# One program for layer 0's feed-forward stage and layer 1's attention

## What is computed

```python
x = layernorm(x + L0_attn(x))     # causal softmax attention
x = layernorm(x + L0_ffn(x))      # ternary weights, silu(x Wu^T) * (x Wg^T), then Wd
x = layernorm(x + L1_attn(x))     # see below
x = layernorm(x + L1_ffn(x))      # silu gate, float32 weights

def L1_attn(x):                   # 16 query heads, 4 key/value heads
    cw = sigmoid(sum(abs(x), axis=-1))
    q = (x * cw) @ Wq
    k, v = split(x @ Wkv)         # keys and values repeated 4 times
    s = q k^T / 4 + alibi(head, -|i-j|)
    s = where(allowed, -1e9, s)   # allowed: |i-j| <= 32, or i < 64, or j < 64
    return softmax(s) v @ Wo + bo
```

## Time and profile before

| | us |
|---|---|
| median of 3 runs (1118.72 to 1123.28) | 1122.21 |
| time of the profiled execution | 1118.5 |
| its span | 1116.8 |
| PE busy in it | 996.9 (89%) |
| DVE busy | 704.0 (63%) |
| ACT busy | 600.9 (54%) |
| POOL busy | 341.0 (31%) |
| mean granted clock of PE | 0.969 |

### The profile page before, as it was taken

How to read it: one execution, slowest core, us unless ns; L and a number is a source line. 1 busy time by engine, 2 the same in 40 slices (tenths; PEclk the granted TensorE clock), 3 DMA queues, 4 the chain that set the end, 5 groups by cost and what they waited for, 6 DMA issues and landing times. The chain is left out here.

```text
span 1116.8 us, 17952 instructions
## 1 busy us (share of the span) xinstructions
PE 996.9 (89%) x6546; PEld 519.4 (47%) x6546; DVE 704.0 (63%) x1549; ACT 600.9 (54%) x1184; POOL 341.0 (31%) x405
## 2 busy tenths in 40 slices
PE   7678999999988999665799999999999999899995
PEld 4332333333334888542233343433333344698885
DVE  2877777778725565466878787777777734225322
ACT  4335666676665334241357777777777676423320
POOL 3031322221211444400252543525234251324331
PEclk9898999999999999977889999999999999999998
DMA  7552120111000000042451331303021000000001
GB/s 248 165 170 68 58 58 16 44 58 58 2 2 1 1 1 1 1 164 66 138 171 41 119 121 40 122 1 122 22 101 36 1 1 1 1 1 20 19 1 38
DMA packets 32979, 64.19 MB, mean 57 GB/s; under 512 B 6079, under 2 KB 22351, under 8 KB 30516
## 3 DMA queue, kind: packets, MB, share of 16 engines
q1 hardware_dynamic: 31004, 58.07, 16.7%
q0 software_dynamic: 1072, 3.80, 1.0%
q10 hardware_dynamic: 816, 1.18, 0.3%
HBM read 50.45 MB, written 12.32 MB: 56 GB/s over the span
## 5 line engine op out<-in xcount | busy, mean ns | idle before, releaser
L932 ACT ACTIVATE prob<-ps 128x512 f32<-128x512 f32 (+6 forms) x896 | 442.8, 537 | 214.8 <-PE ps L978 207.1
L978 PE MATMUL ps<-qop,kop 98*128 98x512 bf16 (+15 forms) x1376 | 302.5, 291 | 21.1 <-ACT prob L932 7.6
L964 PE MATMUL ps<-kop,qop 96*128 96x512 bf16 (+3 forms) x896 | 255.5, 358 | 40.7 <-DVE maxes L871 21.1
L978 PEld LDWEIGHTS ps<-qop,kop 107*128 107x128 bf16 (+2 forms) x1376 | 114.4, 98 | 278.1 <-ACT prob L932 200.9
L1005 PE MATMUL ps<-prob,vst 128*32 128x512 f32 (+4 forms) x1792 | 211.2, 543 | 3.9 <-POOL prob L810 2.6
L871 DVE CUSTOM_DVE_ANT_0 sums<-ps,tri 128x128 bf16<-128x128 f32 (+7 forms) x256 | 183.7, 754 | 43.8 <-PE ps L964 42.5
L871 DVE CUSTOM_DVE_ANT_0 sums<-ps,alibi_table 128x960 bf16<-128x960 f32 x128 | 148.0, 1156 | 77.8 <-PE ps L964 63.4
L810 POOL TENSOR_TENSOR prob<-prob,keep 128x384 int32<-128x384 int32 (+2 forms) x144 | 122.8, 854 | 224.7 <-ACT prob L932 222.2
L1364 PE MATMUL ps<-xs,ffn_parts 128*128 128x512 f32 x640 | 150.4, 392 | 4.5 <-DVE hf L1338 2.3
L871 DVE CUSTOM_DVE_ANT_0 tri<-ps,alibi_table 128x960 bf16<-128x960 f32 x128 | 147.5, 1153 | 3.6 <-PE ps L964 3.6
L1364 PEld LDWEIGHTS ps<-xs,ffn_parts 128*128 128x128 f32 x640 | 119.0, 188 | 29.7 <-DVE hf L1338 3.1
(11 more groups left out here) (99 smaller groups left out, 682.6 us busy)
## 6 DMA issues: line engine op xcount, KB each, us to landing
alibi_table<-in_table SPq DMA_DIRECT2D x32, 464.0 KB, 5.0
qop<-q_parts SPq DMA_DIRECT2D x96, 128.0 KB, 2.7
kop<-k_parts SPq DMA_DIRECT2D x48, 128.0 KB, 2.6
kop<-k_parts SPq DMA_DIRECT2D x48, 96.0 KB
q_parts<-qop SPq DMA_DIRECT2D x8, 384.0 KB, 2.9
q_parts<-kop SPq DMA_DIRECT2D x8, 384.0 KB, 3.5
x<-in_x SPq DMA_DIRECT2D x4, 512.0 KB, 6.0
out<-x SPq DMA_DIRECT2D x4, 512.0 KB, 3.0
```

Of the source, the lines that this page charges most:

```text
L932: nc.scalar.activation(prob[0:rows, q % 2, k % HG, lo % CH:lo % CH + hi - lo], ps[0:rows, t_bank(n, k), lo % CH:lo % CH + hi - lo], ACT.Ex ...
L964: last = nc.tensor.matmul(ps[:, S_BANK + 2 * (k % S_SLOTS) + a // CH, a % CH:a % CH + b - a], qop[0:RD, par, h, i0:i0 + P], kop[0:RD, par, ...
L978: return nc.tensor.matmul(ps[0:rows, bank, a % CH:a % CH + b - a], lhs, rhs, start=start, stop=True, skip_group_check=True)
```

## The change

Layer 0's feed-forward stage and layer 1's attention become one block. `feed_forward` becomes a class `FeedForward` whose engine programs are called at the head of layer 1's attention block; its last down projection, the adding, the last inverse ("root") and the last normalisation ("normal") are steps of layer 1's opening, among the first six maxima. Batch 0 of layer 1's projection is spread behind units 14 to 30 by the dictionary `BRIDGE`, on banks 6 and 7; batch 1 has banks 4, 5 and 6. The order of the units changes too: keys and first query block of a chunk side by side.

The exp on ACT becomes a pow with base 1/e on POOL ("decay", with the 1 added there). For batch 1, "weigh" and "scale" are on ACT (activations Abs with an accumulator, and Copy with a scale). The memory plan is written out by hand (`memory`), so that both stages' buffers fit beside one another: the hidden buffer is four pieces, and xt, xct and vt are one for each batch. Layer 1's projection weights are loaded by SP instead of ACT, at the head of the block. SP's queue is now: weights, constants of buffer 0, (wait for the last gather of attention outputs) four tables, sends 0 to 3, load of group 0, sends 4 and 5, (last hidden tile) constants of buffer 1, (last subtraction) two tables, (last down projection) load of group 1, sends 6 to 11, and on as before. The third part of unit 5 is made at unit 6's step, as before.

```diff
@@ opening_of
+    else:
+        tail = [("down", 0), 0, 1, ("second", 0), ("down", 1), 2, 3, ("second", 1), ("root", 0), 4, 5, ("normal", 0)]
+        out = [maxima[step] if isinstance(step, int) else (*step, 0) for step in tail]
+        maxima = maxima[6:]
     for n, unit in enumerate(maxima):
         out.append(unit)
         upto = [-(-len(behind) * m // (len(maxima) - 2)) for m in (n, n + 1)]
...
+BRIDGE = {14: [("weigh", 0), ("decay", 0)],
+          16: [("divide", 0), ("scale", 0)],
+          20: [("turn", 0), ("turn", 1)],
+          21: [("turn", 2), ("turn", 3)],
+          22: [("weigh", 1), ("decay", 1), ("unit", 0)],
+          23: [("turn", 4), ("turn", 5), ("divide", 1), ("scale", 1)],
+          24: [("turn", 6), ("turn", 7)],
+          25: [("unit", 1)],
+          26: [("unit", 2)],
+          27: [("unit", 3)],
+          28: [("unit", 4)],
+          29: [("unit", 5)],
+          30: [("v", 0)]}
@@ Projection
+            orders = (((KD, 0), (0, 0), (KD, 1), (0, 1), (1, 0), (1, 1)), ((KD, 0), (0, 0), (1, 0), (KD, 1), (0, 1), (1, 1)))
+            self.units = [(b, m, c) for b in range(B) for m, c in orders[b]]
...
+        banks = ((4, 5, 6), (4, 5, 6)) if i == 0 else ((6, 7), (4, 5, 6))
...
+        u, t = units, turns
+        return [("weigh", 2), ("decay", 2), *t[:2], ("divide", 2), ("scale", 2), u[0], *t[2:4], u[1], ("weigh", 3), ("decay", 3),
+                *t[4:6], ("divide", 3), ("scale", 3), u[2], *t[6:], *u[3:], ("v", 1)]
...
+        if self.tenant[step] is not None:
+            self.wait_read(pe, *self.tenant[step])
+        elif self.before is not None and self.bank_of[step] < 6:
+            pe.wait_ge(self.before.prep.added[1], 2 * NC)
+        elif self.before is not None:
+            pe.wait_ge(self.before.prep.n_lo, KD * NC)
...
+        elif what == "decay":
+            tiles = slice(CT * k, CT * k + CT)
+            pool.wait_ge(self.weighed[k // 2], (CT * (k - 1)) if k >= 2 else k + 1)
+            nc.gpsimd.tensor_tensor(self.cw[:, 1, tiles], self.K.inverse_e[:], self.cw[:, 0, tiles], ALU.pow
+                                    ).then_inc(self.cw_exp, 1)
+            pool.wait_ge(self.cw_exp, 2 * k + 1)
+            nc.gpsimd.tensor_scalar(self.cw[:, 2, tiles], self.cw[:, 1, tiles], 1.0, 0.0, ALU.add, ALU.add
+                                    ).then_inc(self.cw_exp, 1)
@@ attend, SP
+                sp.wait_ge(before.prep.gathered, NC)
+                for g in range(HG):
                     load_table(g)
...
-            later = len(proj.units) // 2 + 2 + 2 * (1 - i)
+            later = len(proj.units) // 2 + 2 * (1 - i)
             for u in range(4, later):
                 proj.send(sp, u)
+            if i == 1:
+                sp.wait_ge(before.hid, NC * KE)
+                operands.constants(sp, 1)
+                sp.wait_ge(before.h_lo, NC * KE)
+                for g in range(HG, TABLES):
+                    load_table(g)
+                sp.wait_ge(before.down_full, 2 * NC)
             operands.load(sp, 1)
@@ attend, PE (the same call stands at the head of DVE's, ACT's and POOL's program)
+            if before is not None:
+                before.pe(pe)
             step(-1, opening)
             all_groups(step)
@@ FeedForward
+    def pe(self, pe):
+        self.unit(pe, 0)
+        self.unit(pe, 1)
+        for c in range(NC):
+            for u in range(c * KE + 2, min((c + 1) * KE + 2, NC * KE)):
+                self.unit(pe, u)
+            if c < NC - 1 or self.i == 1:
+                for half in range(2):
+                    self.down(pe, c, half)
...
+        for what, k in self.between(u):
+            self.prep.act(act, what, k)
+        for what, k in self.bridge(u):
+            self.proj.act(act, what, k)
```

More of the change, by code:

```diff
@@ L175, in opening_of @@
 def opening_of(layer, proj):
-    first = proj.steps(0)
+    maxima = [("max", u, 1) for u in range(len(units_of(layer)))]
     behind = proj.steps(1) + [("flush", 0)]
-    maxima = [("max", u, 1) for u in range(len(units_of(layer)))]
     if layer.index == 0:
+        first = proj.steps(0)
         for j, step in enumerate((("unit", 2), ("unit", 4), ("v", 2))):
@@ new lines, in dve_tail, with unit @@
+    def dve_tail(self, dve, what, k):
+        if what == "second":
+            self.add_second(dve, NC - 1, k)
+        elif what == "normal":
+            self.prep.normalise(dve, NC - 1, 1)
+    def unit(self, pe, u):
+        nc, ps, prep, pairs = self.nc, self.K.ps, self.prep, self.pairs
+        c, e = u // KE, u % KE
+        if e == 0 and c >= 2:
+            pe.wait_ge(prep.n_lo, KD * (c + 1))
+        for which, weights, full in ((0, self.wup, self.up_full), (1, self.wgate, prep.gate_full)):
+            if u >= 2:
+                pe.wait_ge(self.silu_done if which == 0 else self.hid, u - 1)
+            n = 0
+            for k in range(KD):
+                for a, b in pairs:
+                    last = nc.tensor.matmul(ps[:, 2 * (u % 2) + which, :],
+                                            weights[a][:, k, e * P:(e + 1) * P],
+                                            prep.xs[:, c % 2, b, k, :],
+                                            start=(n == 0), stop=(n == KD * len(pairs) - 1))
+                    n += 1
+            last.then_inc(full, 1)
+        for what, k in self.between(u):
+            prep.pe(pe, what, k)
+        for what, k in self.bridge(u):
+            self.proj.pe(pe, what, k)
@@ new lines, in down @@
+    def down(self, pe, c, half):
+        nc, pairs = self.nc, self.pairs
+        pe.wait_ge(self.h_lo, KE * (c + 1))
+        if c >= 1:
+            pe.wait_ge(self.prep.added[1], 2 * (c - 1) + half + 1)
+        for j in range(2 * half, 2 * half + 2):
+            n = 0
+            for e in range(KE):
+                for a, b in pairs:
+                    last = nc.tensor.matmul(self.K.ps[:, 4 + half, (j % 2) * D:(j % 2 + 1) * D],
+                                            self.hidden(e, b)[:, j * P:(j + 1) * P], self.wdown[a][:, e, :],
+                                            start=(n == 0), stop=(n == KE * len(pairs) - 1))
+                    n += 1
+        last.then_inc(self.down_full, 1)
@@ new lines, in pe, with pe_tail, alone, _ @@
+    def pe(self, pe):
+        self.unit(pe, 0)
+        self.unit(pe, 1)
+        for c in range(NC):
+            for u in range(c * KE + 2, min((c + 1) * KE + 2, NC * KE)):
+                self.unit(pe, u)
+            if c < NC - 1 or self.i == 1:
+                for half in range(2):
+                    self.down(pe, c, half)
+    def pe_tail(self, pe, what, k):
+        if what == "down":
+            self.down(pe, NC - 1, k)
+def alone(nc, ffn):
+    with ExitStack() as st:
+        block = st.enter_context(nc.Block())
+        @block.sync
+        def _(sp):
+            ffn.sync(sp)
@@ L1391, in _ @@
-            unit(0)
-            unit(1)
-            for c in range(NC):
-                for u in range(c * KE + 2, min((c + 1) * KE + 2, NC * KE)):
-                    unit(u)
-                down(c)
+            ffn.pe(pe)
 def one(n):
```

507 lines of the change are left out of this document (273 added, 234 removed).

## The result

| | kernel before | kernel after |
|---|---|---|
| median, first measurement (5 runs each) | 1121.93 us | 1106.43 us (1099.92 to 1107.78) |
| median, second measurement (9 and 5 runs) | 1122.16 us | 1102.68 us (1100.16 to 1103.88) |
| ratio to before, first | | 0.9853 [0.9832, 0.9875] |
| ratio to before, second | | 0.9825 [0.9805, 0.9845] |
| profiled execution | 1118.5 | 1099.92, span 1098.2, clock 0.973 |

The change makes the kernel faster, by 15.5 us in the first measurement and 19.5 in the second. A median of 1099 us with a range of 1089 to 1112 was predicted: sign and range hold, and the saving is 3.5 to 7.5 us smaller than the 23 forecast.

The account below looks back on a forecast made before the run. TensorE was taken as busy nearly everywhere but for one hole between feed-forward and maxima, the maxima as VectorE's. 29.7 us less up to the first maximum and 6.7 more in the maxima phase gave -23.0, a median near 1099 us, range 1089 to 1112.

Parts of the forecast that it names:

- Up to the first maximum: From unit 31's last matmul to the first maximum: 27.3 us in place of 57.0, so 29.7 us less.
- The stall before turn 6: Units 20 to 24: PE waits for the scaled tokens, 5.8 us of which 4.0 are covered, a stall of 1.8.
- the stall at turn 5: Units 20 to 24: turn 5 needs the bank of unit 0's projection, costing 0.8 us.
- the wait for the last hidden tile: Behind the last unit's matmul: hidden tile, rounding, subtraction and hand-offs hold PE up for 3.0 us.
- the down half: Half of the last down projection ahead of the first maximum: 4.0 us, with +4.0 as bound for half clock.
- The maxima phase: Group 0's maxima on DVE: 43.4 us of work and 6.7 of waits, 50.1 us, so 6.7 us more.
- About 0.35 at each of six units: Maxima phase: DVE waits about 0.35 us at each of six projection units, within the 6.7 us of waits.
- Operands late: Rival: third parts, scaling or sends held up, first maximum waits for "kop<-k_parts"; 15 us saved, 1107; chance 0.15.
- Chains exposed: Rival: each projection unit adds its whole chain to PE, each turn 0.7; 2 us saved, 1120; chance 0.03.
- slower, by the clock: Rival: stalls strewn over units 20 to 31 hold PE at 1.2 GHz; 32 us lost, 1154; chance 0.03.
- Table loads: Rival: ACT's Copy inside the Silu loop brings two loads of 1.28 at six units; 1111 us; chance 0.02.
- The prediction's 5.2 us: Bound on the operands' chain: four third parts could each wait out a POOL subtraction of 1.29; taken as 0.

Follow-up runs that it names:

- experiment 4: e3_flush_early: kernel after with unit 5's second and third part made ahead of the last down projection instead of at unit 6's step; 1102.2 us, 0.9833 to the kernel before.
- Experiments 2 and 3: e2_bridge_last, and that kernel with the whole last down projection, adding and normalisation also ahead of the maxima: 1108.54 us, 0.9894 to the kernel before.
- e1_tail_first: Kernel after with the last down projection, its adding, root and normalisation ahead of all maxima, bridge kept; 1108.11 us, 0.9884 to the kernel before.
- e7_three: Kernel after with unit 5's third part early, turns 6 and 7 one unit later, and chunk 2's normalisation behind the last hidden tile; 1096.2 us, 0.9773.
- e8_keep_busy: Kernel after with 38 idle transposes (20, 12 and 6) in waits of TensorE around the last down projection; 1101.93 us, 0.9829 to the kernel before.
- e2_bridge_last: Kernel after with batch 0's turns, projection units and value turn all behind unit 31, down projection still among the maxima; 1113.8 us, 0.9929 to the kernel before.
- e6_normal_late: Kernel after with chunk 2's normalisation moved from feed-forward unit 29 to the head of the opening; 1103.0 us, 0.9832 to the kernel before.

## Why the prediction was right, and where it was off

**Up to the first maximum: right.** 29.7 us were predicted. The two profiles of before with the slow start have 155.60 and 155.73 from the feed-forward's start to the first maximum, those of after 125.37 and 125.33: 30.3 less (28.4 less than the first profile of before, 153.76). Within it the terms moved both ways. The stall before turn 6 was 2.98 instead of 1.8, since the scaling took 1.92 us beside POOL, inside the bounds of 1.14 to 3.3; the stall at turn 5 (0.8) was absent; the wait for the last hidden tile was 3.64 instead of 3.0; the down half took 5.42 up to the first maximum instead of 4.0, on the way to the 8.0 of its bound for half clock. Against that the turns were cheaper: two in a row occupy PE for 0.79 (438.04 to 438.83), where I took 1.20 from the row's length, so 1.6 less over four pairs. A row's length overstates: the next row starts before it ends. Units 26 to 29 took 3.57 each against 3.7. The 0.9 us that are left of the balance are about the two waits of PE, 0.75 and 0.26 us, that the kernel before has inside unit 24 (at 433.24) and ahead of the down projection of chunk 2. In the kernel after they are gone, and the prediction had not counted them. Some 3.2 us were so put too low and some 4 us too high: that this part came out within 0.6 us is in part luck.

**The maxima phase: this is the step that failed.** "Together 6.7, so 50.1 us" was 54.5 (54.51 and 54.49 in the two profiles of after, against 43.46). DVE's waits in it are 10.15 instead of 6.7, and its work about 1 us more than 43.4. By its terms: the start 0.73 (0.6), the second down half 1.62 (2.2), three units in a row 1.60 (1.8) were right. "About 0.35 at each of six units" was not: the three units that stand apart cost 0.79, 2.56 and 0.80, 4.15 in place of 2.1. Three waits (0.39, 0.49, 0.49) for a maximum's product that stands behind four transposes at the lower clock were not in the sum. Nor was unit 5's third part, 0.68 waited and 0.69 of work, though the change's description says that it is made at unit 6's step; experiment 4 takes it out of the phase. Most of this was to be seen in the phase before: the lines above have waits of 0.38 and 0.49 and the third part there, and DVE waited 0.86 for the cast of the first unit. The prediction wrote that phase as maxima, remainders and "the rest waits", and then put new waits in the place of the rest instead of reading it.

Of the 4.4 us some 3 are rows at the lower clock (1.37 behind the transposes, some 1.8 of the 2.56), in a phase for which the prediction's own showed 0.89, while the sum took PE's durations at full clock. The 1.8 is no fixed price: of the eleven profiles of one-block kernels three (e1_tail_first, e7_three, e8_keep_busy) have no projection unit at the lower clock in this phase and eight have one or two, of 3.05 to 3.55 us, not always the same unit; the three of the kernel before have none.

**The rivals.** *Operands late* did not happen, though the first measurement's 1106.43 lies at its price (1107) and just outside the forecast's own range of 1094 to 1106: there is no wait for "kop<-k_parts". Unit 3's third part was done at 468.79, 12.8 us behind the end of chunk 2's down projection (13.3 predicted). Experiments 2 and 3 show that the mechanism is real when the bridge is later (5.24 and 1.76). *Chains exposed* and *slower, by the clock* were wrong as well: PE runs 447.9 to 474.9 without a gap at clock 1.00. *Table loads* in the silu loop there are none, and the one that moved is hidden, as the timeline of ACT in the kernel after shows:

```profile
534.99 1.28 ACT L1005 ACT_TABLE_LOAD   x1
```

It runs 6 us before the first exp's matmul at 542.31.

**The Trainium skill** ("SBUF — State Buffer", section "Who interferes with whom") says that a VectorE instruction with two SBUF inputs contends with a GpSimd instruction that reads SBUF, and that the order of issue decides which of the two is held up. The prediction's 5.2 us took only the case in which VectorE is. Two third parts met a subtraction of POOL, by the timeline of DVE in the kernel after,

```profile
457.98 0.78 DVE L485 TENSOR_TENSOR qop<-staging,qop 64x512 bf16<-64x512 f32 x1
...
462.83 0.67 DVE L485 TENSOR_TENSOR qop<-staging,qop 128x512 bf16<-128x512 f32 x1
```

and that of POOL:

```profile
456.92 1.29 POOL L1367 TENSOR_TENSOR hs<-hf,hs 128x512 fp32r<-128x512 f32 x1 [14.13 <-ACT hs L1393]
...
463.04 1.63 POOL L1367 TENSOR_TENSOR hs<-hf,hs 128x512 fp32r<-128x512 f32 x1 [2.74 <-ACT hs L1393]
```

The first began 0.23 us before POOL's subtraction ended and took 0.78 us, where the next one of its shape, beside an idle POOL, took 0.67 (464.69). The second began ahead of POOL's subtraction and took 0.67, and the subtraction took 1.63 instead of 1.29. So the one that began second was the longer one, by 0.11 and 0.34 us: the trace agrees with the page on who pays. The 5.2 us did not come, since none of the four third parts of this chain began early in a subtraction of POOL. In experiment 4 the same meeting lengthened POOL's work by 0.45 us, on PE's path.

**The offset.** The profile of after (1099.92) lies 3.9 below the median of its ten executions, as that of before lay 3.7 below its own; adding 3.7 to the forecast of a profile held. From profile to profile the change saved 18.6 us, or 19.2 in the joined stretch beside the two profiles of before with the slow start, where 23.0 were forecast; 30.3 less 11.0 is the same 19.2, so the miss is the maxima phase.

**The other signs.** The first maximum came at 484.0 (482 forecast), 9.1 us behind the last unit's matmul (7 forecast), and the slices that were to be at 8 or 9 are one 8 and three 7.

## What to carry to other kernels

When two stages are joined, look first at what the long-latency chain of the second (here cast, send, load of the keys) can run beside: with the projection in one piece ahead of the last down projection two thirds of the gain were there, and spreading it finely paid only together with the early use of its result. In a phase where TensorE waits between short bursts, cost its instructions at the lower clock for the sum, not only for the range. When a phase stays but changes, list its old waits one by one before putting new ones in their place. And take an instruction's cost from the start of the next one, not from its row's length (0.79 against 1.20 us for two turns here).

## What the runs showed of the hardware

- The same three waits of PE (2.44, 0.70 to 0.86 and 1.08 us) left the clock full in one profile and at its lower level in thirteen, which costs 1.9 to 2.8 us in the 16 matmuls behind them. Likewise waits of 2.90 and 2.98 us were followed by a down half of 4.06 and 4.07 in e2_bridge_last and e6_normal_late, and one of 2.98 by a half of 5.59 in e7_three. Behind 3.64 us it was 5.57 (kernel after), behind 4.09 us 6.51 (e3_flush_early), and behind 1.45 us, with idle transposes ahead, 4.07 (e8_keep_busy).
- A scaling of four 128x256 tiles on DVE took 1.92 us beside a subtraction on POOL, and a normalisation of the same shape 2.35 beside one, which itself took 1.44 instead of 1.29, and 1.38 without.
- Of a subtraction with two SBUF inputs on DVE and one on POOL that met, the one that began second took longer: 0.78 instead of 0.67 us on DVE, 1.63 instead of 1.29 us on POOL.
- Layer 0's program, the same in all kernels, brought the feed-forward's start anywhere from 358.61 to 361.45 us.
